# Four edits to the second block of a four-layer kernel: where its stand-by products, splits, statistics and weight sums lie

## The chip, the core and the metric

The kernel runs on one core of one Trainium2 chip. The time is device microseconds for one execution. The kernel before has three timed runs: 600.94 us as their median, 597.98 us the lowest, 601.21 us the highest. Lower is better.

The engines of a core run side by side and wait for each other with semaphores: TensorE (PE; its weight loads are PEld), VectorE (DVE), ScalarE (ACT), GpSimd (POOL) and SyncE (SP), which issues most DMAs. PE writes into eight PSUM banks of 128x512 f32. Each engine goes through its own list in order.

## The reference, cut to what matters

x has 2048 tokens (4 batches of 512) of 128 numbers, in 16 tiles of 128 tokens. Four layers follow each other, each a cross attention to 32 context tokens per batch and a feed-forward part:

```
x = x + L0_xattn(ln(x));  x = x + L0_ffn(ln(x))    # top-2 of 8 experts, GELU
x = x + L1_xattn(ln(x));  x = x + L1_ffn(ln(x))    # top-2 of 8 experts, ReLU
x = x + L2_xattn(ln(x));  x = x + L2_ffn(ln(x))    # quantised weights, convolution, SiLU
x = x + L3_xattn(ln(x));  x = x + L3_ffn(ln(x))    # top-2 of 8 experts, SiLU gate
```

The change lies in layer 1. Its attention is one head of 128: scores of the tokens against the context's keys, softmax over 32, and the sum of the values. Its experts are computed for every token and weighted by a gate G that is zero except for the two chosen:

```
h = relu(einsum('th,ehf->etf', xf, W1) + b1[:, None, :])
y = einsum('etf,efh->eth', h, W2) + b2[:, None, :]
out = einsum('te,eth->th', gate, y)
```

Layer 2's feed-forward part scales each weight matrix by the mean of its absolute values before it rounds it to -1, 0 or 1:

```
scale = 1.0 / jnp.clip(jnp.mean(jnp.abs(w)), 1e-05)
return jnp.clip(jnp.round(w * scale), -1, 1) / scale
```

## The kernel before, in words

`experts(0)` ends layer 0 with a loop over tiles sorted by expert. Then `second_block()`, which each engine has in its own version, does layer 1 and the whole attention of layer 2. The order of each engine's work is written out by hand; nothing is planned or moved by a scheduler.

The second block works in two halves of eight tiles. The first half goes through layer 1's attention before the dense part starts: DVE normalises (`ln_scale` raises `xa_ready`), PE turns the tiles (`tokens1`), ACT copies them to SBUF, PE makes scores (`scores1`), DVE and ACT the softmax (`scores1`, `exponents1`, `shares1`), PE turns the shares and multiplies by the values (`turns1`, `values1`), and DVE adds the result to X (`add1`, two times 128x512). Between these PE makes keys and values of layer 2 (`projected`, `summed`).

DVE then normalises X again for the dense experts, and PE turns these tiles into banks 4 and 5 (`tokens_d`). The products with W1 are made in three passes of a rounded part and a rest, so the tokens are needed as two parts too: `high` (ACT, rounded copy of the bank into XHL), `whole` (ACT, plain copy of the bank into XTF, which the trace calls gb), and `low` (DVE, whole minus high). Of these, `up_d` needs high and low, and `logits_d` (the gate's product) needs the two whole copies of its half.

The dense part is 32 units, `u = 0..31`: group `u // 8` of four tiles, expert `u % 8`. In unit u PE does `up_d(u)` (six 128x512 passes, lines 2016 to 2018), then what the list has at that unit, then `down_d(u-1)` (line 2027, sixteen records). ACT does `hidden1(u)` (ReLU), and DVE `combine1(u)` (line 1602, adds gate times result to X). The second half's attention and its tokens for the dense part are placed among units 2 to 15: its turned tokens come in at units 5 (`tokens1(2)`, `tokens1(3)`) and 14 (`tokens_d(2)`, `tokens_d(3)`), its logits at unit 15.

The means of layer 2's weights are three steps: DVE sums absolute values (`weight_sums`, two reductions), PE adds over the partitions into bank 7, and DVE reads bank 7 (`weight_scales`, which raises `fs_read` twice). POOL waits for `fs_read` 2 and then prepares the weights for layer 2; PE waits for the end of that (`fs_ready`) ahead of layer 2's feed-forward part only.

## Time and profile before

| | us |
|---|---|
| median of three runs | 600.94 |
| lowest, highest | 597.98, 601.21 |
| the profiled execution | 604.28 |
| its span | 602.5 |
| PE busy in the span | 543.9 (90%) |
| DVE busy | 401.4 (67%) |
| ACT busy | 239.3 (40%) |
| POOL busy | 280.1 (46%) |

The span runs from the first to the last instruction of the profiled execution, and 1.78 us of its time lie around it. The execution is 3.34 us above the median of the timed runs. The granted clock of TensorE was 0.949 of full speed on average over the span. The second block starts at about 186 us, its units run from 208 to about 342 us.

A timeline row reads: start, duration, engine, line, operation, output and inputs, shapes, how many, and in brackets how long the engine idled before it and what ended that. PE's ends are modelled and overlap with the next record, so the time that a group takes of PE is better read from start to start. A matmul in f32 shows as two records, a transpose as one.

### The profile page before, as it was taken

To read this page: it belongs to the slowest core of one execution; us is meant where nothing else is said; L and a number is where in the kernel's file an instruction comes from. 1 tells how busy PE (TensorE), PEld (TensorE's weight loads), DVE (VectorE), ACT (ScalarE), POOL (GpSimd) and SP (SyncE) were. 2 spreads that over 40 slices of the span, in tenths; PEclk is the share of its full clock that TensorE was granted. 3 is DMA by queue.
4 is the path that set the end of the run, shared out by engine and by line. 5 is a ranking of instruction groups with operands and counts; after the bars stand their busy time and mean duration, and the time that the engine had idled before them with its cause. 6 is when DMAs were issued, how large, how long until landed. Compare 5 with 4: busy or idle time off the path is not lost.

```text
span 602.5 us, 12300 instructions
## 1 busy us (share of the span) xinstructions
PE 543.9 (90%) x3794; PEld 458.7 (76%) x3809; DVE 401.4 (67%) x1443; ACT 239.3 (40%) x551; POOL 280.1 (46%) x521
## 2 busy tenths in 40 slices
PE   5999984769999799999999999999996897999992
PEld 3678744669997498889987877767773697899992
DVE  8978853333356795465789899988887654555573
ACT  3555503345553543434444334365521222343330
POOL 4474378867657106910000050664526688644332
PEclk9999865999998999989999999999998798999997
DMA  9999012222253100000000450004001222111233
GB/s 302 377 328 274 13 53 67 68 62 75 71 167 104 64 1 1 2 0 1 1 2 0 141 140 2 1 1 141 1 1 45 67 70 58 54 46 52 79 110 122
DMA packets 48153, 47.65 MB, mean 79 GB/s; under 512 B 6471, under 2 KB 37604, under 8 KB 47943
## 3 DMA queue, kind: packets, MB, share of 16 engines
q1 hardware_dynamic: 43558, 37.68, 21.3%
q0 software_dynamic: 4544, 9.38, 4.7%
q8 instruction: 22, 0.36, 0.2%
q14 instruction: 29, 0.23, 0.1%
HBM read 27.53 MB, written 19.51 MB: 78 GB/s over the span
## 4 chain that ended last, share of the span: by engine, by line
PE 58%; DVE 18%; issue 11%; SPq 8%; ACT 2%; another core or an unknown queue 1%; DMA 1%; DVEq 0%; POOL 0%; POOLq 0%; ACTq 0%
PE bank L2453 18%; PE bank L2466 10%; PE bank L2027 7%; SPq L474 4%; SPq L468 2%; PE bank L2016 2%; PE bank L2017 2%; PE bank L2018 2%; PE bank L2441 2%; PE bank L2310 2%; PE bank L2223 2%; SPq L463 1%; PE bank L2268 1%; DVE X L1602 1%
## 5 line engine op out<-in xcount | busy, mean ns | idle before, releaser
L2453 PE MATMUL bank<-xT,wcur 128*128 128x128 f32 x936 | 122.7, 282 | 14.1 <-ACT xT L903 10.5
L2453 PEld LDWEIGHTS bank<-xT,wcur 128*128 128x128 f32 x936 | 114.6, 197 | 17.3 <-issue 9.4
L706 POOL DMA_INDIRECT yt<-Y,dest_i x62 | 60.3, 973 | 59.6 <-ACT Y L919 39.3
L645 POOL TENSOR_SCALAR var_eps<-mv 128x4 f32<-128x4 f32 (+2 forms) x12 | 2.9, 238 | 165.4 <-DVEq L1846 93.5
L690 POOL DMA_INDIRECT xw<-XW,slot_i x64 | 63.1, 986 | 24.6 <-issue 13.0
L1458 DVE COPY wcur<-WA 128x512 f32 x78 | 35.2, 452 | 51.1 <-PE bank L2453 37.3
L987 ACT ACTIVATE hT<-bank,b_cols 128x512 f32<-128x512 f32 x64 | 44.0, 688 | 61.4 <-PE bank L2018 60.8
L2027 PE MATMUL bank<-WC,hT 128*128 128x128 f32 x512 | 64.4, 281 | 0.0
L2027 PEld LDWEIGHTS bank<-WC,hT 128*128 128x128 f32 x512 | 62.0, 196 | 1.6 <-issue 0.2
L1473 DVE TENSOR_TENSOR hT<-gb,bank 128x512 f32<-128x512 f32 x39 | 26.8, 688 | 50.5 <-ACT gb L908 44.2
L1602 DVE SCALAR_TENSOR_TENSOR X<-bank,G,X 128x128 f32<-128x128 f32 x128 | 35.9, 345 | 29.9 <-PE bank L2027 23.5
L908 ACT ACTIVATE gb<-bank 128x512 f32<-128x512 f32 x39 | 23.3, 598 | 54.8 <-PE bank L2453 49.3
L2466 PE MATMUL bank<-WB,hT 128*128 x312 | 41.7, 276 | 0.4 <-issue 0.2
L2466 PE MATMUL bank<-WA,hT 128*128 x312 | 40.9, 275 | 0.0
L2466 PEld LDWEIGHTS bank<-WB,hT 128*128 128x128 f32 x312 | 38.2, 192 | 1.0 <-issue 0.9
L2466 PEld LDWEIGHTS bank<-WA,hT 128*128 128x128 f32 x312 | 37.8, 192 | 0.0
L2268 PE MATMUL bank<-M,XT 128*128 128x512 f32 x64 | 34.9, 628 | 0.1
L908 ACT ACTIVATE hT<-bank 128x512 f32<-128x512 f32 x39 | 23.3, 598 | 27.4 <-PE bank L2453 20.9
L2310 PE MATMUL bank<-VB,YT 128*128 128x36 f32 x256 | 31.9, 271 | 0.0
L2310 PEld LDWEIGHTS bank<-VB,YT 128*128 128x128 f32 x256 | 31.1, 192 | 0.4
L826 ACT ACTIVATE YT<-YT 128x512 f32<-128x512 f32 x32 | 20.2, 632 | 24.4 <-DVE YT L1255 24.4
L919 ACT ACTIVATE Y<-bank 128x128 f32<-128x128 f32 x62 | 17.3, 279 | 31.8 <-PE bank L2466 23.7
(407 smaller groups left out, 1185.6 us busy)
## 6 DMA issues: line engine op xcount, KB each, us to landing
xw<-pad_rows SPq DMA_DIRECT2D x34, 260.0 KB, 4.2
xrow<-xw SPq DMA_DIRECT2D x78, 65.0 KB
WA<-in_fc_dram SPq DMA_DIRECT2D x16, 256.0 KB, 4.3
YT<-yt SPq DMA_DIRECT2D x16, 256.0 KB, 3.2
WA<-in_pj_dram SPq DMA_DIRECT2D x8, 256.0 KB, 5.9
WB<-in_fc_dram SPq DMA_DIRECT2D x8, 256.0 KB, 5.3
WB<-in_pj_dram SPq DMA_DIRECT2D x8, 256.0 KB, 6.5
X<-in_x_dram SPq DMA_DIRECT2D x2, 512.0 KB, 4.2
```

Source lines behind the costliest of these rows:

```text
L690: pool.indirect_dma_start(out=xw_dram, out_offset=bass.IndirectOffsetOnAxis(ap=slot_i[:, choice, tile:tile + 1], axis=0), in_=XW[:, tile, ...
L706: pool.indirect_dma_start(out=yt_dram, out_offset=bass.IndirectOffsetOnAxis(ap=dest_i[:, t:t + 1], axis=0), in_=y_slot(layer, t), in_offse ...
L908: act.activation(dst[:, 0:nc_f, :], bank[s % 2][:, 0:f].rearrange("p (c t) -> p c t", c=nc_f), L["act"]).then_inc(ex_act, 1)
L987: act.activation(hT[F1C * (u % 2) + c][:, :, :], four(bank[F1C * (u % 2) + c]), ACT.Relu, bias=b1_cols[:, F1C * e + c:F1C * e + c + 1]).th ...
L1458: ins = dve.tensor_copy(wcur[:, t % RING, i * width:(i + 1) * width], w[:, bass.ds(e, 1), :].rearrange("p a f -> p (a f)"))
L1473: dve.tensor_tensor(hT[s][:, :, :], gb[:, s % 2, :, :], bank[2 + s % 2][:, :].rearrange("p (c t) -> p c t", c=4), ALU.mult).then_inc(ex_mu ...
L1602: dve.scalar_tensor_tensor(out=X[:, t, :], in0=bank[4 + u % 2][:, j * D:(j + 1) * D], scalar=G[:, t, e:e + 1], in1=X[:, t, :], op0=ALU.mul ...
L2027: ins = pe.matmul(bank[4 + u % 2][:, j * D:(j + 1) * D], hT[F1C * (u % 2) + c][:, j, :], DOWN1[:, e, c * D:(c + 1) * D], start=(c == 0), s ...
L2268: pe.matmul(bank[s % 2][:, :], XT[:, s, :], M[:, b, :], start=True, stop=False)
L2310: ins = pe.matmul(bank[4 + j % 2][:, c * VW:(c + 1) * VW], PT[:, j % 2, c, :], VB[:, b, c, :], start=True, stop=True)
L2453: ins = pe.matmul(dst, wcur[:, s4, at:at + P], xT[s4 % 2][:, :], start=True, stop=True)
L2466: ins = pe.matmul(y, hT[s4][:, c, :], dn[:, bass.ds(e, 1), c * P:(c + 1) * P].rearrange("p a d -> p (a d)"), start=(c == 0), stop=(c == nc ...
```

## The change

1. PE does four more products of ones (`warm(4, 3)`, 128x512 bf16 into bank 3, which nobody reads) at the head of the second block, behind the last products of the loop and ahead of the first wait for `xa_ready`.
2. `low` reads the turned tokens from their PSUM bank, and waits for `xd_high` and no longer for `xd_out`. `whole` now waits for the `low` of the same group (`xd_low`). On ACT, the two `high` come first and then the two `whole`, in both halves.
3. At the head, DVE's statistics of the first four tiles (`ln_stats`) come between `add1(0)` and `add1(1)`, those of the other four behind `add1(1)`.
4. DVE's `weight_sums` moves from ahead of `gates1(0)` to unit 3, `weight_scales` from unit 3 to unit 6 behind `shares1(1)`. PE's product of the sums moves from unit 3 to unit 6 behind `scores1(1)`. PE's wait for `fs_read` moves from ahead of `tokens1(3)` (unit 5) to ahead of `turns1(2)` (unit 9).

```
             def whole(i, src):
+                act.wait_ge(xd_low, i + 1)
                 act.activation(XTF[:, i % 2 * BT:(i % 2 + 1) * BT, :], four(src), ACT.Copy).then_inc(xd_out, 1)
...
                 for i in range(2):
                     high(i, bank[4 + i])
+                for i in range(2):
                     whole(i, bank[4 + i])
...
                     if u == 14:
                         high(2, bank[6])
+                        high(3, bank[7])
                         whole(2, bank[6])
-                        high(3, bank[7])
                         whole(3, bank[7])
...
             def low(i):
-                dve.wait_ge(xd_out, i + 1)
-                dve.tensor_tensor(XLO[i], XTF[:, i % 2 * BT:(i % 2 + 1) * BT, :].rearrange("p t c -> p (t c)"),
-                                  XH[i].bitcast(F32), ALU.subtract).then_inc(xd_low, 1)
+                dve.wait_ge(xd_high, i + 1)
+                dve.tensor_tensor(XLO[i], bank[4 + i][:, :], XH[i].bitcast(F32), ALU.subtract).then_inc(xd_low, 1)
...
-                add1(0, bank[3])
-                add1(1, bank[0])
-                dve.wait_ge(a1_added, GB)
-                layer_norm(half(0), XNR[:, 0:GT, :], xd_ready)
+                for b, src in ((0, 3), (1, 0)):
+                    add1(b, bank[src])
+                    dve.wait_ge(a1_added, b + 1)
+                    ln_stats(everything[b * BT:(b + 1) * BT], b * BT)
+                ln_aggregate(half(0))
+                ln_rstd(GT)
+                ln_scale(half(0), XNR[:, 0:GT, :], xd_ready)
...
-                weight_sums()
                 gates1(0, bank[5])
...
                     if u == 3:
-                        weight_scales()
+                        weight_sums()
...
                     if u == 6:
                         shares1(1)
+                        weight_scales()
...
             def second_block():
+                warm(4, 3)
                 for b in range(GB):
...
-                    if u == 3:
-                        weight_sums()
                     if u == 5:
                         pe.wait_ge(s2_act, 9)
                         tokens1(2, bank[6])
-                        pe.wait_ge(fs_read, 1)
                         tokens1(3, bank[7])
                     if u == 6:
                         scores1(1, bank[6])
+                        weight_sums()
                     if u == 9:
+                        pe.wait_ge(fs_read, 1)
                         turns1(2, bank[7])
```

The next two pieces show ACT's list at units 14 and 15, with the waits of each row. XHL is the rounded copy (`high`), gb the whole one, hT the hidden layer of `hidden1`. First the kernel before:

```order
L987 ACTIVATE hT0<-bank0,b1_cols 128x512 [waits d_dn,d_up]
L987 ACTIVATE hT1<-bank1,b1_cols 128x512 [waits d_dn,d_up]
L972 ACTIVATE XHL<-bank6 128x512 [waits xd_mm]
L975 ACTIVATE gb<-bank6 128x512
L972 ACTIVATE XHL<-bank7 128x512 [waits xd_mm]
L975 ACTIVATE gb<-bank7 128x512
L987 ACTIVATE hT2<-bank2,b1_cols 128x512 [waits d_dn,d_up]
L987 ACTIVATE hT3<-bank3,b1_cols 128x512 [waits d_dn,d_up]
```

And the changed kernel at the same place:

```order
L988 ACTIVATE hT0<-bank0,b1_cols 128x512 [waits d_dn,d_up]
L988 ACTIVATE hT1<-bank1,b1_cols 128x512 [waits d_dn,d_up]
L972 ACTIVATE XHL<-bank6 128x512 [waits xd_mm]
L972 ACTIVATE XHL<-bank7 128x512 [waits xd_mm]
L976 ACTIVATE gb<-bank6 128x512 [waits xd_low]
L976 ACTIVATE gb<-bank7 128x512 [waits xd_low]
L988 ACTIVATE hT2<-bank2,b1_cols 128x512 [waits d_dn,d_up]
L988 ACTIVATE hT3<-bank3,b1_cols 128x512 [waits d_dn,d_up]
```

The whole copies now stand behind both rounded ones and wait for DVE; the hidden rows of unit 15 stay behind them.

On PE, these rows of the kernel before are the ends of unit 5's first products, the turned tokens of the second half, and the head of `down_d(4)`:

```order
L2018 MATMUL bank3<-XHL,W1L 128x512
L1967 MATMUL bank6<-ident,XW 128x128 [waits xa_ready,s2_act]
L1967 MATMUL bank6<-ident,XW 128x128 [waits xa_ready] x3
L1967 MATMUL bank7<-ident,XW 128x128 [waits xa_ready,fs_read]
L1967 MATMUL bank7<-ident,XW 128x128 [waits xa_ready] x3
L2027 MATMUL bank4<-WC,hT0 128x128 [waits d_added,d_act]
```

The changed kernel has there:

```order
L2022 MATMUL bank3<-XHL,W1L 128x512
L1971 MATMUL bank6<-ident,XW 128x128 [waits xa_ready,s2_act]
L1971 MATMUL bank6<-ident,XW 128x128 [waits xa_ready] x3
L1971 MATMUL bank7<-ident,XW 128x128 [waits xa_ready] x4
L2031 MATMUL bank4<-WC,hT0 128x128 [waits d_added,d_act]
```

The wait for `fs_read` has left the second four transposes.

## Rows read from the trace of the kernel before

**Rows 1.** The page, its first line.

```profile
span 602.5 us, 12300 instructions
```

**Rows 2.** Timeline of DVE, second sum and statistics: start, us, engine, line, operation.

```profile
199.51 0.69 DVE L1571 TENSOR_TENSOR X<-X,bank 128x512 f32<-128x512 f32 x1 [0.20 <-PE bank L1987]
200.23 1.65 DVE L1122 BATCH_NORM_STATS2 stats<-X 128x6 f32<-128x128 f32 x8
```

**Rows 3.** Timeline of ACT, the two rounded copies ahead of unit 0.

```profile
206.34 0.60 ACT L972 ACTIVATE XHL<-bank 128x512 fp32r<-128x512 f32 x1 [0.68 <-PE bank L1993]
...
207.37 0.60 ACT L972 ACTIVATE XHL<-bank 128x512 fp32r<-128x512 f32 x1
```

**Rows 4.** Timeline of DVE, the first `low`.

```profile
207.46 0.69 DVE L1575 TENSOR_TENSOR XHL<-gb,XHL 128x512 fp32r<-128x512 f32 x1 [0.51 <-ACT gb L975]
```

**Rows 5.** Timeline of PE, head of unit 0 and its logits.

```profile
208.41 0.47 PE L2016 MATMUL bank<-XHL,W1H 128*128 128x512 f32 x1 [1.08 <-DVE XHL L1575]
...
210.76 1.85 PE L2001 MATMUL bank<-w,gb 128*128 128x8 f32 x16
```

**Rows 6.** Timeline of PE, unit 5: turned tokens of the second half.

```profile
228.70 0.60 PE L1967 MATMUL bank<-ident,XW 128*128 128x128 f32 x4
230.67 0.66 PE L1967 MATMUL bank<-ident,XW 128*128 128x128 f32 x4 [1.38 <-DVE wmean L1626]
231.16 1.95 PE L2027 MATMUL bank<-WC,hT 128*128 128x128 f32 x16
```

**Rows 7.** Timeline of DVE: a weight sum, and the scaling of the second half.

```profile
213.67 0.69 DVE L1620 TENSOR_REDUCE wmean<-w_s 128x1 f32<-128x512 f32 x1 [0.16 <-DVE X L1528]
...
227.38 2.14 DVE L1146 TENSOR_SCALAR XW<-X,mv,rstd 128x128 f32<-128x128 f32 x8
```

**Rows 8.** Timeline of PE, units 14 and 15: turned tokens, `down_d(13)`, logits.

```profile
269.62 1.03 PE L1993 MATMUL bank<-ident,XW 128*128 128x128 f32 x8
270.50 1.95 PE L2027 MATMUL bank<-WC,hT 128*128 128x128 f32 x16
...
273.68 1.85 PE L2001 MATMUL bank<-w,gb 128*128 128x8 f32 x16
```

**Rows 9.** Timeline of DVE, `combine1(13)` and the two `low` behind it.

```profile
272.48 1.13 DVE L1602 SCALAR_TENSOR_TENSOR X<-bank,G,X 128x128 f32<-128x128 f32 x4 [2.94 <-PE bank L2027]
273.52 1.28 DVE L1575 TENSOR_TENSOR XHL<-gb,XHL 128x512 fp32r<-128x512 f32 x2
```

**Rows 10.** Timeline of POOL: head of the weights' preparation, and one piece of it.

```profile
230.93 0.70 POOL L784 TENSOR_SCALAR w_s<-w_s,wmean 128x512 f32<-128x512 f32 x1 [32.15 <-DVE wmean L1628]
...
239.90 1.27 POOL L791 TENSOR_TENSOR Z<-w_s,Z 128x512 f32<-128x512 f32 x1
```

**Rows 11.** Timeline of DVE: the same subtraction in each half, and `combine1(11)`.

```profile
193.24 0.59 DVE L1557 TENSOR_TENSOR WC<-WC,l_max 128x256 f32<-128x256 f32 x1
...
240.07 1.38 DVE L1557 TENSOR_TENSOR WC<-WC,l_max 128x256 f32<-128x256 f32 x1
...
265.31 1.13 DVE L1602 SCALAR_TENSOR_TENSOR X<-bank,G,X 128x128 f32<-128x128 f32 x4 [3.47 <-PE bank L2027]
```

**Rows 12.** Timeline of PE, head of the second block and the second pair of projections.

```profile
187.19 2.26 PE L1967 MATMUL bank<-ident,XW 128*128 128x128 f32 x8 [0.94 <-DVE XW L1146]
...
192.03 3.76 PE L2052 MATMUL bank<-wkv_s,w 128*128 128x512 f32 x4
...
199.40 1.98 PE L2052 MATMUL bank<-wkv_s,w 128*128 128x512 f32 x4
```

**Rows 13.** Stretches of PE: us, busy (records), granted clock, DMA share, GB/s.

```profile
190.00:191.00 1.00, 1.00 (x7) 0.50 0.00 0
...
262.00:264.00 2.00, 2.00 (x11) 0.50 0.00 0
```

**Rows 14.** Groups by line, 200 to 420 us: products of ones.

```profile
L1907 PE MATMUL bank<-ones_bf 128*128 128x512 bf16 x6 | 1.5, 379 | 0.0
```

**Rows 15.** Timeline of PE, `down_d(11)` at the lower clock.

```profile
261.53 3.67 PE L2027 MATMUL bank<-WC,hT 128*128 128x128 f32 x16
```

More of the change, by code:

```diff
@@ L974, in whole @@
             def whole(i, src):
+                act.wait_ge(xd_low, i + 1)
                 act.activation(XTF[:, i % 2 * BT:(i % 2 + 1) * BT, :], four(src), ACT.Copy).then_inc(xd_out, 1)
@@ L1008, in second_block @@
                     high(i, bank[4 + i])
+                for i in range(2):
                     whole(i, bank[4 + i])
@@ L1031, in second_block @@
                         high(2, bank[6])
+                        high(3, bank[7])
                         whole(2, bank[6])
-                        high(3, bank[7])
                         whole(3, bank[7])
@@ L1573, in low @@
             def low(i):
-                dve.wait_ge(xd_out, i + 1)
-                dve.tensor_tensor(XLO[i], XTF[:, i % 2 * BT:(i % 2 + 1) * BT, :].rearrange("p t c -> p (t c)"),
-                                  XH[i].bitcast(F32), ALU.subtract).then_inc(xd_low, 1)
+                dve.wait_ge(xd_high, i + 1)
+                dve.tensor_tensor(XLO[i], bank[4 + i][:, :], XH[i].bitcast(F32), ALU.subtract).then_inc(xd_low, 1)
             def gates1(g, src):
@@ L1632, in second_block @@
                 shares1(0)
-                add1(0, bank[3])
-                add1(1, bank[0])
-                dve.wait_ge(a1_added, GB)
-                layer_norm(half(0), XNR[:, 0:GT, :], xd_ready)
+                for b, src in ((0, 3), (1, 0)):
+                    add1(b, bank[src])
+                    dve.wait_ge(a1_added, b + 1)
+                    ln_stats(everything[b * BT:(b + 1) * BT], b * BT)
+                ln_aggregate(half(0))
+                ln_rstd(GT)
+                ln_scale(half(0), XNR[:, 0:GT, :], xd_ready)
                 low(0)
@@ L1640, in second_block @@
                 combine_second(0, 1)
-                weight_sums()
                 gates1(0, bank[5])
@@ L1652, in second_block @@
                     if u == 3:
-                        weight_scales()
+                        weight_sums()
                     if u == 5:
@@ L1657, in second_block @@
                         shares1(1)
+                        weight_scales()
                     if u == 9:
@@ L2113, in second_block @@
             def second_block():
+                warm(4, 3)
                 for b in range(GB):
@@ L2136, in second_block @@
                         pe.wait_ge(d_read, 1)
-                    if u == 3:
-                        weight_sums()
                     if u == 5:
@@ L2141, in second_block @@
                         tokens1(2, bank[6])
-                        pe.wait_ge(fs_read, 1)
                         tokens1(3, bank[7])
@@ L2145, in second_block @@
                         scores1(1, bank[6])
+                        weight_sums()
                     if u == 9:
+                        pe.wait_ge(fs_read, 1)
                         turns1(2, bank[7])
```

## The prediction

> **What bounds the kernel now.** I read the page first, for the span of 602.5 us [rows 1], then who waited for whom on PE between 180 and 345 us, then the chain of waits over the same stretch, and last the timelines of PE, DVE and ACT. The reader is to see that the second block runs as one chain. Ahead of unit 0 it goes back and forth between DVE, ACT and PE; from unit 0 on it is PE alone, whose records follow each other without a gap except at a few places. So a microsecond of DVE, ACT or POOL counts there only where PE waits for it, and one that PE loses or gains at such a place goes through to the end: the transfers that follow are issued behind results of this chain. Two waits of PE in this stretch are touched: 1.08 us ahead of unit 0, for the first low part [rows 5], and 1.38 us in unit 5, put down to DVE's reading of the weight sums [rows 6]. And there is a place with no wait today that the change makes into one: the logits of unit 15 [rows 8].
>
> The time of the profiled execution is 604.28 us, 1.78 us more than its span. The sum below is made against it; the median of the runs is 3.34 us lower, and I carry the difference over to 600.94 us. A difference under 0.5% (3.0 us) is what a measurement of this kernel can't tell from none.
>
> **Statistics between the sums.** DVE sat idle for 0.20 us between the two additions and then did eight statistics in 1.65 us [rows 2]. Four of them (0.82 us) now start in that hole, and the second addition comes behind them. All instructions stay, only the hole closes, less one more hand-over of about 0.03 us: a gain of 0.15 us, bounds 0 and 0.20 us.
>
> **Low parts from PSUM.** The first rounded copy ends at 206.34 + 0.60 = 206.94 us [rows 3], and DVE is free at 207.46 - 0.51 = 206.95 us [rows 4]. Today `low(0)` starts at 207.46 us since it waits for the whole copy. It will start at about 206.98 us: 0.48 us sooner. A 128x512 addition with one operand in PSUM took 0.69 us [rows 2], and so did `low` with two in SBUF [rows 4], so its length stays. PE's head of unit 0 follows `low(0)` and moves by the same 0.48 us; its turned tokens are in the banks before that. With the statistics, PE starts unit 0 0.6 us earlier (bounds 0.4 and 0.7). The whole copies go to the back: whole 1 waits for `low(1)`, which waits for the second rounded copy (ends 207.37 + 0.60 = 207.97 us [rows 3]), so about 207.97 + 0.03 + 0.69 + 0.05 + 0.60 = 209.35 us. The first logits need it at 210.76 - 0.6 = 210.2 us [rows 5]: hidden, with 0.8 us to spare.
>
> The Trainium skill (VectorE: DVE Perf Modes, on the TRN2 errata) gives a DVE operation a fixed part that is 62 cycles, 0.065 us, longer with its source in PSUM than in SBUF. By it this gain would be 0.42 us; the rows above show no such difference, so 0.48 us stays.
>
> **Weight sums among units.** The two reductions, 0.69 us each and about 1.3 us together [rows 7], leave the place ahead of the gates. DVE is late at that time, so its scaling of the second half, which ends at 227.38 + 2.14 = 229.52 us [rows 7], comes 1.3 us sooner. The two reductions then stand in unit 3 and the reading in unit 6, where DVE waits for PE anyway. PE turned four tiles at 228.70 us, waited, turned the other four and began `down_d(4)` at 231.16 us: 2.46 us from start to start. In unit 14 the same eight took 270.50 - 269.62 = 0.88 us [rows 8]. With no wait for `fs_read`, and the scaling done by 228.2 us, unit 5 takes 0.88 us too, so PE gains 1.6 us (lower bound 1.2 us, if only the part up to 229.52 us goes; upper bound 1.6). PE's small product moves from unit 3 to unit 6: nothing. The wait for `fs_read` at unit 9 comes three units after DVE's reading in unit 6: nothing.
>
> POOL's preparation starts at 230.93 us [rows 10] and moves from unit 3's end to unit 6's; its result is read in layer 2's feed-forward part, long after. But it comes to lie beside DVE's statistics and scaling of units 9 to 12. One subtraction took 1.38 us instead of 0.59 us while POOL's product was at work [rows 10, 11]. Ahead of unit 11's `combine1` DVE idles 3.47 us [rows 11], so one or two such stretches of 0.8 us are hidden: zero, and 0.8 us as upper bound.
>
> The Trainium skill (GPSIMD Engine Reference, Specifications) says that POOL shares its SBUF interfaces with VectorE and that instructions with two SBUF inputs contend; the two rows of the subtraction agree. By it `low` from PSUM, with one SBUF input, would no longer be exposed. It changes no term.
>
> **The whole copies of the second half.** This is the term that speaks against the change. In unit 14 today ACT makes all four copies as soon as the tokens are turned, so PE finds them done at 273.68 us [rows 8]. Now the whole copies wait for `low(2)` and `low(3)`, and these have not moved: on DVE they stand behind `combine1(13)`, which starts at 272.48 us since it waits for `down_d(13)`, and run from 273.52 to 274.80 us [rows 9]. The first low ends at about 274.2 us, whole 2 at 274.85, whole 3, with 0.60 us a copy, at 275.45 us. PE's logits wait for it: 275.5 us in place of 273.68 us, a loss of 1.8 us (bounds 1.6 and 2.1). Behind the waiting copies on ACT stand the hidden rows of unit 15, to about 276.8 us; PE wants them in unit 16, after the logits and `down_d(14)`, so that costs nothing more. Behind the waiting logits on PE stands everything else of the block.
>
> **The products of ones.** Before the head of the second block PE idled 0.94 us, then turned eight tiles in 2.26 us at the pace of DVE's scaling [rows 12]. After that its granted clock fell to 0.50, the level of 1.2 GHz [rows 13], and four 128x512 records took 3.76 us that took 1.98 us at the upper level [rows 12]. Six products of ones took 1.5 us [rows 14], so four take 1.0 us. They fill the gap of 0.94 us, and at most 0.1 us sticks out, which the pace of DVE swallows: cost zero. Whether they keep the clock up is not in the trace. If they do, the keys' product ends 1.8 us sooner and what follows, with the shares now the last to come, follows by 1.8 us. Bounds: 0 and 1.8 us gain. The clock fell also at 261.5 us with PE never idle [rows 13, 15], so gaps are not its only cause, and the turned tokens stay sparse; I take 0.
>
> The Trainium skill (TensorE: Matmul & The Clock Gate, the part on the HAM clock gate) says that the clock follows how busy PE was of late. By it ones in the gap make a fall less likely, which is the second case below.
>
> **The sum.** -0.6 - 1.6 + 1.8 = -0.4 us: 603.9 us for an execution like the profiled one, 600.5 us against the median.
>
> **The rivals.**
> - The ones hold the clock at the head. For it: the fall came right behind the gap. Against it: PE's work there stays thin up to the keys. -0.4 - 1.8 = -2.2 us: 598.7 us.
> - The clock falls behind the new gap, the case on the slower side. PE would idle 1.8 us and then do sixteen records of only eight columns (1.85 us [rows 8]). For it: the fall at the head came after 0.94 us of idling and thin work. Against it: around unit 0 there were 1.08 us of idling [rows 5] with no fall. `down_d` at the lower clock took 3.67 us, not 1.95 us [rows 15, 8], so one such fall costs 1.7 us: +1.3 us, 602.2 us. It decides whenever the ones don't win the same sum back.
> - No new gap: the whole copies come in time after all, and the change does just what it says. For it: the first half, where they do. Against it: the place of `low(2)` in DVE's list. -0.6 - 1.6 = -2.2 us: 598.7 us, or 596.9 us with the clock held.
> - POOL's work, moved to units 7 to 14, holds DVE up by more than it idles, and PE waits for scaled tiles in unit 14. For it: 1.38 against 0.59 us. Against it: DVE's 3.47 us of slack. +0.8 us on the sum: 601.3 us.
>
> **How the numbers follow.** Chances: forecast 0.42; clock held 0.27; clock lost in the new gap 0.16; no new gap 0.10; POOL 0.05. The timed runs of before spread over 3.2 us by themselves, so each case carries about 1.5 us to either side. The range from 597.3 to 603.2 us takes in the clock held below and the clock lost above. Faster by over 0.5% (under 597.9 us): the last part of "no new gap" and the lower edge of "clock held", 0.17. Slower by over 0.5% (above 603.9 us): the upper edge of "clock lost", 0.09. Within: 0.74.
>
> **What would show it.** PE's head of unit 0 should follow the first rounded copy by about 1.0 us, where it was 1.47 us. In unit 5 the eight turned tokens should follow each other. In unit 15 there should be an idle of PE of 1.8 us ahead of the logits, ended by ACT's whole copy, with ACT itself waiting for `low`. The granted clock between 190 and 197 us shows what the ones did, that behind unit 15 what the gap did. Wrong would be: no wait ahead of the logits of unit 15, or a wait still left in unit 5.

## The result, and the profile after

| | before | after |
|---|---|---|
| median of the runs compared, us | 599.46 (4) | 607.1 (4) |
| ratio after to before, 95% interval | | 1.0125 [1.008, 1.017] |
| the profiled execution, us | 604.28 | 605.64 |
| its span | 602.5 | 603.9 |

The changed kernel is slower by 1.25%, about 7.5 us. The forecast was 600.5 us with a range up to 603.2 us, and 0.09 for slower by over 0.5%. It was wrong. On some chips a few executions of every kernel take over 1.5% longer than its fastest; no ratio and no row below is taken from such an execution.

The page's first line, which answers to [rows 1]:

```profile
span 603.9 us, 12309 instructions
```

The span is only 1.4 us longer, but that hides the loss: the part behind the second block took 251.7 us here and 258.4 in the profile of before. It took between 246 and 259 us in the profiles of this study, in kernels that don't differ there, so it says nothing about the change. I therefore cut PE's timeline and compare the stretches between the cuts. "Head" runs from the end of the first loop to the first `up_d(0)`.

| us | head | `up_d(0)` to `down_d(4)` | to `down_d(13)` | to the logits of unit 15 | to the first tile turned behind the block | sum |
|---|---|---|---|---|---|---|
| before | 22.2 | 22.7 | 39.3 | 3.2 | 70.4 | 157.9 |
| after | 23.7 | 20.9 | 42.4 | 6.3 | 70.6 | 164.0 |

So the block is 6.1 us longer, and the loss sits in the third and the fourth stretch, with some in the head. The second gains.

Timeline of PE after, unit 5, where [rows 6] had a wait:

```profile
232.07 1.03 PE L1971 MATMUL bank<-ident,XW 128*128 128x128 f32 x8
232.94 1.95 PE L2031 MATMUL bank<-WC,hT 128*128 128x128 f32 x16
```

All eight tiles in a row, 0.87 us from start to start instead of 2.46. This is as forecast. Timeline of PE after, units 14 and 15, which answers to [rows 8]:

```profile
272.07 0.30 PE L1997 MATMUL bank<-ident,XW 128*128 128x128 f32 x1 [1.91 <-DVE XW L1148]
274.18 1.39 PE L1997 MATMUL bank<-ident,XW 128*128 128x128 f32 x7 [1.81 <-DVE XW L1148]
275.37 3.26 PE L2031 MATMUL bank<-WC,hT 128*128 128x128 f32 x16
...
281.67 1.95 PE L2005 MATMUL bank<-w,gb 128*128 128x8 f32 x16 [1.65 <-ACT gb L976]
```

Two waits for DVE's scaled tokens, 1.91 and 1.81 us, stand where there was none. `down_d(13)` takes 3.26 us instead of 1.95, and then comes the wait for the whole copies, 1.65 us. Stretches of PE after (us, busy, then granted clock, DMA share, GB/s):

```profile
272.00:274.00 2.00, 0.30 (x1) 0.14 (x1) 2.00 (x3) 0.00 (x0) 1.73 (x1) 1.00 0.00 0
274.00:276.00 2.00, 1.82 (x10) 1.76 (x11) 1.93 (x8) 0.99 (x2) 0.00 (x0) 0.67 0.00 0
276.00:278.00 2.00, 2.00 (x12) 2.00 (x11) 0.00 (x0) 0.21 (x1) 0.00 (x0) 0.50 0.00 0
```

Behind the wait the clock went to the level of 1.2 GHz. Why DVE was late is in its own timeline after, around the square root of the normalization:

```profile
261.64 0.98 DVE L1136 TENSOR_SCALAR var_eps<-mv 128x8 f32<-128x8 f32 x1
...
264.71 0.17 DVE L1141 TENSOR_TENSOR y_squared<-rstd 128x8 f32<-128x8 f32 x1
264.91 4.36 DVE L1142 SCALAR_TENSOR_TENSOR minus_half_vyy<-var_eps,y_squared 128x8 f32<-128x8 f32 x1
...
271.16 3.74 DVE L1148 TENSOR_SCALAR XW<-X,mv,rstd 128x128 f32<-128x128 f32 x8
```

An operation on 128x8 elements stands for 4.36 us; its neighbour of the same size in the row above takes 0.17. The scaling takes 3.74 us; it took 2.14 [rows 7]. Timeline of POOL after, at that time:

```profile
263.38 1.28 POOL L793 TENSOR_TENSOR w1c_l<-Z,w1c_h 128x512 fp32r<-128x512 f32 x1
264.74 7.10 POOL L796 TENSOR_SCALAR mfill<-WC 35x2048 bf16<-35x2048 int32 x1
271.90 1.83 POOL L797 MEMSET mfill<- 3x2048 bf16 x1
```

Behind the weights' preparation POOL makes a mask for layer 2, in one operation of 7.10 us, and fills three rows of it with ones in a memset of 1.83 us. The reader is to see that DVE's operation starts 0.17 us behind the first. The memset lies beside the scaling; the timeline of DVE after for 271.9 to 273.7 us alone:

```profile
271.16 2.72 DVE L1148 TENSOR_SCALAR XW<-X,mv,rstd 128x128 f32<-128x128 f32 x4
```

The first four of the eight scalings take 2.72 us, the other four only 1.0 us more. The first four end at 273.88 us, 0.15 us behind the memset's end, and PE's second wait ends at 274.18 us, 0.45 us behind it. So the long operation makes PE's first wait, and the memset most of the longer scaling and the second wait. In the trace of before the same operation stands here:

```profile
250.10 7.09 POOL L796 TENSOR_SCALAR mfill<-WC 35x2048 bf16<-35x2048 int32 x1
```

and DVE did this beside it and behind it:

```profile
253.91 1.12 DVE L1602 SCALAR_TENSOR_TENSOR X<-bank,G,X 128x128 f32<-128x128 f32 x4 [4.22 <-PE bank L2027]
254.95 1.27 DVE L1571 TENSOR_TENSOR X<-X,bank 128x512 f32<-128x512 f32 x2
256.26 1.65 DVE L1122 BATCH_NORM_STATS2 stats<-X 128x6 f32<-128x128 f32 x8
...
259.65 0.17 DVE L1134 TENSOR_SCALAR var_eps<-mv 128x8 f32<-128x8 f32 x1
```

Nothing was held: the combines and sums have one operand in PSUM, and the square root came 2.5 us after the long operation and 0.6 us after the memset was done. Counted from the end of the first loop, the fourth edit moved POOL's list some 13 us later, and with it the mask onto the square root.

The head after: timelines of ACT and PE, one row each, which answer to [rows 3, 5].

```profile
210.42 0.60 ACT L972 ACTIVATE XHL<-bank 128x512 fp32r<-128x512 f32 x1 [0.64 <-PE bank L1997]
```

```profile
212.00 0.47 PE L2020 MATMUL bank<-XHL,W1H 128*128 128x512 f32 x1 [0.59 <-DVE XHL L1577]
```

PE starts 0.98 us behind the end of the first rounded copy, as forecast (1.0, was 1.47). From the first of the turned tokens to the start of unit 0 it took 2.72 us (209.28 to 212.00), where it was 3.20. That the head is 1.6 us longer all the same comes from its beginning, where PE waited 1.70 us for ACT's copies of the turned tokens. None of the seven other profiles with the ones in the kernel has that wait, c_after among them, which differs from this kernel by its bound checks only. So the wait is this execution's own. The head of c_after is as long (23.9 us) for another reason: the values, the second projection and the value sum ran at the lower clock there (3.02, 3.78 and 3.56 us, where before had 2.05, 1.98 and 1.98).

### The profile page after: what moved, and what is told of

Its sections match the earlier page's. It is cut to its first block, busy times and chain, and to the rows that moved or that the text cites. A ratio compares the mean times of both kernels' runs of the same rounds, so it can differ in the third digit from the quotient of the medians.

```text
span 603.9 us, 12309 instructions
## 1 busy us (share of the span) xinstructions
PE 546.4 (90%) x3798; PEld 459.9 (76%) x3813; DVE 408.6 (68%) x1443; ACT 236.9 (39%) x551; POOL 281.8 (47%) x521
## 4 chain that ended last, share of the span: by engine, by line
PE 67%; DVE 22%; another core or an unknown queue 4%; issue 3%; ACT 2%; DMA 1%; SPq 0%; POOL 0%; DVEq 0%; POOLq 0%; ACTq 0%
PE bank L2457 18%; PE bank L2470 11%; PE bank L2031 7%; PE bank L2314 4%; PE bank L2272 3%; PE bank L2303 2%; PE bank L2020 2%; PE bank L2021 2%; PE bank L2022 2%; PE bank L2227 1%; PE bank L2445 1%; PE bank L1911 1%; DVE X L1603 1%; DVE minus_half_vyy L1142 1%
## 5 line engine op out<-in xcount | busy, mean ns | idle before, releaser
L2457 PE MATMUL bank<-xT,wcur 128*128 128x128 f32 x936 | 120.9, 280 | 9.4 <-ACT xT L903 6.5
L2457 PEld LDWEIGHTS bank<-xT,wcur 128*128 128x128 f32 x936 | 113.3, 196 | 11.9 <-issue 9.3
L1254 DVE TENSOR_REDUCE smax<-bank 128x16 f32<-128x512 f32 x32 | 22.0, 689 | 12.3 <-PE bank L2274 5.0
```

Of the source, the lines that this page charges most:

```text
L2457: ins = pe.matmul(dst, wcur[:, s4, at:at + P], xT[s4 % 2][:, :], start=True, stop=True)
```

## The experiments

Every kernel here carries 64 bound checks of loaded numbers on SyncE that the two kernels above leave out; `c_before` and `c_after` are the kernels before and after with them and nothing else. Names with a_ start from the changed kernel, names with b_ from the one before. The ratio is always to the kernel before on the same chip. The chips differ (before ran at 575.8 to 604.5 us), so I compare ratios, and microseconds only of kernels run on the same chip. The intervals don't hold all of the doubt: from the medians of all executions c_after would be 1.0118, a_no_ones 1.0078, b_edit4 1.0041 and b_edit4_mid 0.9960.

| kernel | what | ratio | interval |
|---|---|---|---|
| c_before | nothing | 0.9994 | [0.9955, 1.0034] |
| c_after | the whole change | 1.0088 | [1.0051, 1.0125] |
| a_no_ones | change without the ones | 1.0129 | [1.0084, 1.0173] |
| a_weights_back | without edit 4 | 1.0086 | [1.0058, 1.0113] |
| a_copies_back | second half's copies as before | 1.0076 | [1.0050, 1.0102] |
| a_mask_early | mask ahead of POOL's wait | 1.0146 | [1.0095, 1.0196] |
| a_mask_mid | mask in units 3 to 6 | 0.9996 | [0.9947, 1.0046] |
| b_edit4 | edit 4 alone | 1.0073 | [1.0036, 1.0109] |
| b_edit4_mid | edit 4, mask in units 3 to 6 | 0.9974 | [0.9939, 1.0009] |
| b_edit4_split | edit 4, mask in 8 pieces | 0.9986 | [0.9959, 1.0012] |
| b_copies | second half's copies alone | 1.0064 | [1.0016, 1.0111] |
| b_copies_look | the same | 1.0040 | [1.0012, 1.0068] |
| b_copies_order | their order alone | 0.9971 | [0.9927, 1.0015] |
| b_edit3 | low parts, statistics in the head | 0.9972 | [0.9938, 1.0007] |
| b_ones | the ones alone | 0.9983 | [0.9944, 1.0022] |
| head_only | ones and b_edit3 | 1.0038 | [0.9988, 1.0089] |
| best2 | change, mask mid, copies back | 0.9940 | [0.9904, 0.9977] |
| best2_no_ones | the same without ones | 0.9948 | [0.9909, 0.9987] |

The stretches of the block (the same cuts) in the profiles that matter below:

| us | head | to `down_d(4)` | to `down_d(13)` | to the logits | behind them | sum |
|---|---|---|---|---|---|---|
| c_before | 22.7 | 22.9 | 37.7 | 3.2 | 70.4 | 156.9 |
| c_after | 23.9 | 20.9 | 42.8 | 5.8 | 72.1 | 165.5 |
| a_no_ones | 21.4 | 20.9 | 42.8 | 5.9 | 72.1 | 163.1 |
| a_weights_back | 22.5 | 22.3 | 39.3 | 5.0 | 70.5 | 159.7 |
| a_mask_mid | 21.5 | 20.9 | 39.6 | 5.0 | 70.5 | 157.5 |
| b_edit4 | 22.1 | 20.9 | 42.8 | 4.7 | 70.4 | 161.0 |
| b_edit4_mid | 22.0 | 20.9 | 37.9 | 3.2 | 70.4 | 154.5 |
| b_edit4_split | 21.8 | 27.1 | 37.9 | 3.2 | 70.4 | 160.4 |
| b_copies_look | 22.0 | 27.2 | 37.7 | 5.0 | 73.8 | 165.7 |

The first two stretches swing by some microseconds with where the clock falls: the 27 us of the last two kernels, which ran on one chip in one go, hold a second fall in units 0 to 3. The third stretch is 1.6 us longer where the clock fell ahead of unit 14 (before, a_weights_back and a_mask_mid). So one profile is worth no more than that, and the verdicts rest on the ratios.

From b_copies, best2 and best2_no_ones no row is read.

**First, what each part of the change is worth.** c_after:

> The changed kernel with 64 bound checks of the loaded waits put on SyncE, the form that all runs of this study share; nothing else differs. Theory A (the loss lies in the second block): as slow against before as the changed kernel, 1.0125, some 7 us, and in the profile PE waits about 4 us for the scaled tiles of unit 14, 1.7 us for the whole copies of unit 15, and 1.7 us for ACT's copy at the head. Rival (the loss lies in the loops, by chance or by where code lies): the second block takes within 1 us of the 158 us it took before, from the end of the loop to layer 2's first turned tokens.

Measured 1.0088, with waits where the profile after has them: 0.30 and 1.81 us in unit 14 (the first is short since the clock had fallen from 261.6 to 265.0 us and PE came later), 1.65 us for the copies, and a fall of the clock behind the second and the third. The wait of 1.7 us at the head was not there.

a_weights_back undoes the fourth edit:

```
 combine_second(0, 1)
+weight_sums()
 gates1(0, bank[5])
...
-if u == 3: weight_sums()
+if u == 3: weight_scales()
```

> The changed kernel with edit 4 undone (weight sums, their reading and PE's wait where they were before). Theory A1 (POOL's preparation, moved beside DVE's statistics and scaling of units 10 and 11, holds DVE up): DVE's 128x8 operations of unit 10 are back at 0.17 us each, the scaling at 2.1 us, the waits of PE in unit 14 (4.3 us) are gone, the wait of 1.4 us in unit 5 is back: 3 to 4 us faster than the changed kernel. Rival (only the copies and the head cost): 1.6 us slower than the changed kernel.

The wait in unit 14 was gone and 0.93 us were back in unit 5, yet the ratio stayed at 1.0086, where 3 to 4 us were expected back. By the medians, on the same chip, it was 2.5 us faster than c_after. So the fourth edit is not the only loss. The block of its profile is 159.7 us, 2 to 3 us over the two of the kernel before (157.9 and 156.9); that is 0.3 to 0.5%, and the rest of the 0.86% is not found in it. a_copies_back puts the second half's copies back:

```
-                act.wait_ge(xd_low, i + 1)
+                if i < 2:
+                    act.wait_ge(xd_low, i + 1)
```

> The changed kernel with the low parts and whole copies of the second half made as before (in the first half as changed). Theory A2: PE's wait ahead of unit 15's logits goes from 1.65 us to nothing, and the time falls by 1.7 us; the waits in unit 14 stay. Rival: the logits then wait for something else, DVE's or ACT's late work, and the time stays.

No wait ahead of the logits, the two of unit 14 (1.92 and 1.81 us) still there, 1.0076. The 1.7 us expected are 0.3%; the ratio is 0.12% below that of c_after, and the intervals tell that neither from 0.3% nor from nothing.

**The mask moved too early.** a_mask_early puts POOL's mask ahead of its wait for the weights' means:

```
+pool.wait_ge(in_mask3, 16)
+link(pool.tensor_scalar(mfill[0:PARTS + K, :], mask3_i, 0, FILL, ALU.is_equal, ALU.mult))
 pool.wait_ge(fs_read, 2)
```

> The changed kernel with POOL's two mask operations (7.1 and 1.8 us) moved from behind to ahead of its wait for the weight means, where POOL idles. Theory A1, in the form that the long mask operation holds DVE's ports: the 4.36 us that one 128x8 operation of DVE took in unit 10 fall to under 1.2 us, the scaling is back at 2.1 us, PE waits under 1 us in unit 14, and the time falls by 4 to 5 us. Rival (it is the three taps' products, not the mask): DVE stays late by over 3 us and the time falls by under 1.5 us.

It has the highest ratio of all, 1.0146, and it was the most telling run. Its input arrives when DVE normalizes in the head. Timelines of POOL, DVE and PE of that kernel:

```profile
198.75 7.12 POOL L783 TENSOR_SCALAR mfill<-WC 35x2048 bf16<-35x2048 int32 x1 [3.24 <-DMA WC<-in_mask_dram]
205.92 1.79 POOL L784 MEMSET mfill<- 3x2048 bf16 x1
```

```profile
199.07 6.83 DVE L1137 TENSOR_SCALAR var_eps<-mv 128x8 f32<-128x8 f32 x1
205.93 1.82 DVE L1139 TENSOR_SCALAR seed_bits<-var_eps 128x8 int32<-128x8 int32 x1
```

```profile
209.99 2.27 PE L1998 MATMUL bank<-ident,XW 128*128 128x128 f32 x8 [8.93 <-DVE XW L1149]
```

The hold went with the mask to another place. The first 128x8 operation ends at 205.90 us, the mask at 205.87. The second ends at 207.75 us, the memset at 207.71. POOL's operations, not something in unit 14, hold DVE, and here each holds it to its end.

**The controls, and the change repaired.** c_before and a_no_ones:

> The kernel before, with the 64 bound checks of the loaded numbers on SyncE that every kernel of these experiments carries; nothing else differs from before. It prices the checks: if they cost nothing, the ratio to before is 1.000 within 0.3% and the four kernels run so far are 0.8 to 1.5% slow through the change alone, even with most of it undone. My theory: the checks cost 2 to 4 us (SyncE issues the gathers of the weights in the first loop, whose start they delay), so this one reads 594 to 596 beside 591.8, and the control of the change stands 3 to 5 us behind it. Block (end of the first loop to the last layer's first turned tokens) 157 to 159 us as before, no wait of TensorE ahead of unit 14.

No cost of the checks shows (0.9994, at most 0.34% by the interval, or 2.0 us); my theory of 2 to 4 us fell.

```
-                warm(4, 3)
```

> The changed kernel without the ones behind the first loop. Theory (the ones only move the fall of the clock: held through the first scores, it falls when TensorE waits 1.8 us for the shares): head as in before (scores 3.0 us, first projection 3.76 us at 1.2 GHz, values at full clock), unit 0 starts 22.0 to 22.6 us behind the loop beside 23.9 in the control, time 0 to 1.5 us below the control. Rival (the ones hold the clock and gain): unit 0 later than in the control and the time 1 us above it. The waits of TensorE for the scaled tokens in unit 14 stay, 4 us in all.

1.0129, so the ones are not the loss. best2 takes the changed kernel, the second half's copies as before, and the mask behind a wait that ends in unit 3 (`d_added` counts the combines):

```
+pool.wait_ge(d_added, 16)
+link(pool.tensor_scalar(mfill[0:PARTS + K, :], mask3_i, 0, FILL, ALU.is_equal, ALU.mult))
 pool.wait_ge(fs_read, 2)
```

> The changed kernel with GpSimd's mask operations (the one of 7.1 us) put into units 3 to 6, where the vector engine runs only its combines, instead of behind the weight scales, and the second half's whole copies as before. Theory: the operation of 128x8 in the normalization's square root takes about 0.2 us again beside 4.4, the scaling 2.1 beside 3.7, TensorE waits for nothing ahead of unit 14's transposes nor ahead of the logits, and TensorE waits no more for the weight means in unit 5: block 157 to 158 us plus what the head costs, 5 to 6 us below the control of the change. Rival (any combine beside the 7.1 us operation is held as long): TensorE waits 1 to 4 us for a combine in units 3 to 6, and the gain is half that.

> The same as best2 without the ones. If the ones only move the fall of the clock, it is 0 to 1.5 us faster than best2 and the fastest of the four, 1.5 to 2.5 us below the control of before; if they gain, it is about 1 us slower than best2.

0.9940 and 0.9948: both faster than before, by 0.6 and 0.5%, and the best of the study. The ones make no difference that shows.

**One part at a time, on the kernel before.** b_edit4 and b_edit4_mid:

> The kernel before with the fourth edit alone: weight sums of TensorE in unit 6 instead of 3, its wait for them ahead of unit 9, the vector engine's sums in unit 3 and scales in unit 6; head, copies and ones as before. Theory: unit 5 gains 1.6 us (d4 20.9 us behind unit 0 instead of 22.8), GpSimd's 7.1 us operation then holds the square root's 128x8 operation of the vector engine for about 4.3 us and stretches its scaling to 3.7, TensorE waits 1.9 + 1.8 us in unit 14 and runs on at 1.2 GHz for some 4 us: block 2 to 4 us over before, ratio 1.004 to 1.008. Rival (the loss of the whole change sits in the head or the copies): ratio 0.997 to 1.000, no wait in unit 14.

> The same with GpSimd's mask operations in units 3 to 6, ahead of its work on the weight means. Theory: unit 5 keeps its 1.6 us, unit 14 waits for nothing, the square root's operation takes 0.2 us: block 1.5 to 2 us under before, ratio 0.996 to 0.998. Rival (GpSimd's short weight scales hold the vector engine as well): TensorE waits 1 to 2 us in unit 14 and the ratio is 1.000.

1.0073 and 0.9974, both within the numbers of the theory. Timeline of DVE in b_edit4, where the mask starts at 261.62 us:

```profile
261.59 0.17 DVE L1139 TENSOR_TENSOR y_squared<-rstd 128x8 f32<-128x8 f32 x1
261.79 4.36 DVE L1140 SCALAR_TENSOR_TENSOR minus_half_vyy<-var_eps,y_squared 128x8 f32<-128x8 f32 x1
...
268.03 3.74 DVE L1146 TENSOR_SCALAR XW<-X,mv,rstd 128x128 f32<-128x128 f32 x8
```

In b_edit4_mid the timeline of DVE and that of PE at unit 14:

```profile
263.18 0.17 DVE L1141 SCALAR_TENSOR_TENSOR minus_half_vyy<-var_eps,y_squared 128x8 f32<-128x8 f32 x1
...
265.22 2.13 DVE L1147 TENSOR_SCALAR XW<-X,mv,rstd 128x128 f32<-128x128 f32 x8
```

```profile
268.26 1.03 PE L1994 MATMUL bank<-ident,XW 128*128 128x128 f32 x8
```

POOL's two mask operations, moved by some 30 us, are worth 1.0% (1.0073 against 0.9974), some 6 us; by the medians 0.8%. The block is 161.0 us in the one and 154.5 in the other. What is left of edit 4 in the trace is the gain of unit 5; 0.9974 itself can't be told from nothing. Beside the long operation DVE now had combines and the two reductions (0.68 us each), and none of them was held.

> The kernel before with the low parts of the first half taken from PSUM, their whole copies behind them, and the statistics between the values' sums; no ones, second half and weight sums as before. Theory: unit 0 starts 0.6 to 1.2 us earlier (a_no_ones had it 21.4 us behind the loop, before 22.2 to 22.7), the ratio is 0.998 to 1.000. Rival (the head costs what the run with the weights back seemed to lose beyond its copies, some 3 us): ratio 1.005.

> The kernel before with the ones alone behind the first loop. Theory (the ones move the fall of the clock from the first projection to the values and the second projection, where it is as long): ratio 1.000 to 1.002, unit 0 at 22 to 24 us behind the loop, TensorE waits about 1.8 us for the shares. Rival (they gain): unit 0 below 21 us behind the loop and a ratio of 0.997.

0.9972 and 0.9983, neither told from nothing. For the ones, the timelines of PE at the head of c_before and of head_only, which has them:

```profile
188.47 2.36 PE L1967 MATMUL bank<-ident,XW 128*128 128x128 f32 x8 [0.97 <-DVE XW L1146]
190.61 3.46 PE L1974 MATMUL bank<-M,gb 128*128 128x32 f32 x16
193.89 3.66 PE L2052 MATMUL bank<-wkv_s,w 128*128 128x512 f32 x4
...
201.16 1.98 PE L2052 MATMUL bank<-wkv_s,w 128*128 128x512 f32 x4
```

```profile
187.71 1.03 PE L1917 MATMUL bank<-ones_bf 128*128 128x512 bf16 x4
188.84 2.26 PE L1977 MATMUL bank<-ident,XW 128*128 128x128 f32 x8
190.94 1.93 PE L1984 MATMUL bank<-M,gb 128*128 128x32 f32 x16
192.70 1.96 PE L2062 MATMUL bank<-wkv_s,w 128*128 128x512 f32 x4
196.44 1.05 PE L1991 MATMUL bank<-ident,WC 128*32 128x128 f32 x8 [1.77 <-DVE WC L1569]
197.72 3.43 PE L1997 MATMUL bank<-V,hT 32*128 32x128 f32 x16 [0.24 <-ACT hT L967]
201.08 3.78 PE L2062 MATMUL bank<-wkv_s,w 128*128 128x512 f32 x4
```

The scores and the first projection run at full clock, 1.93 and 1.96 us. PE then has to wait 1.77 us for the shares, since DVE and ACT make the softmax no sooner, and now the clock falls, so that the values and the second projection pay. The fall was moved and not removed. So it was in five of the eight profiles with the ones. In the other three (after, a_mask_early, a_mask_mid) the clock fell 4 to 5 us behind the loop, hardly later than in c_before (3.0). The same move as in head_only happened in b_edit3, which has no ones but in whose execution the gap of 0.97 us was not there either. In the profile of the changed kernel itself the clock fell already at the scores.

> The changed kernel's head alone (ones, low parts of the first half from PSUM, statistics between the sums), with the second half's copies and the weight sums as before. Theory: the parts add up, 0.9972 and 0.9983 alone, so 0.995 to 0.999, unit 0 at 22.5 us behind the loop. Rival (together they cost what the run with the weights back lost beyond its copies): 1.003 or more, with rounded copies late at the scalar engine.

1.0038 with an interval that takes in both; it decides nothing.

**The rest: the copies.** The parts did not add up to 1.25%, so b_copies makes the second half's copies as the change has them, b_copies_order only their order, and a_mask_mid is the whole change with the mask in units 3 to 6.

```
+                if i >= 2:
+                    act.wait_ge(xd_low, i + 1)
                 act.activation(XTF[:, i % 2 * BT:(i % 2 + 1) * BT, :], four(src), ACT.Copy).then_inc(xd_out, 1)
```

with `low` of the second half from PSUM.

> The kernel before with the second half's copies alone as the change has them: both rounded copies first, low parts from PSUM, whole copies behind the low parts. Theory (the wait ahead of the logits and nothing more): TensorE waits 1.65 us for the whole copies ahead of unit 15's logits, the block is 1.6 to 1.8 us longer than before's, ratio 1.002 to 1.004, no fall of the clock behind it. Rival (the copies cost the 0.5 to 0.8% that is missing): a fall of the clock in unit 16 or a later wait, block 3.5 us longer, ratio 1.005 to 1.008.

> The kernel before with the scalar engine's four copies of the second half in the order rounded, rounded, whole, whole, the low parts still from the whole copies in SBUF. If the order alone makes the wait, TensorE waits 1 us or more ahead of the logits and the ratio is 1.002 or more; theory (the wait for the low parts makes it): the last whole copy ends where it ended before, no wait ahead of the logits, ratio 1.000.

```
                         high(2, bank[6])
+                        high(3, bank[7])
                         whole(2, bank[6])
-                        high(3, bank[7])
                         whole(3, bank[7])
```

> The whole changed kernel with GpSimd's mask operations moved to units 3 to 6, nothing else. Theory: the wait of unit 14 goes (with the vector engine's square root at 0.2 us), the wait of 1.65 us ahead of the logits stays and no clock fall follows it; block 1.5 to 2 us longer than best2's, ratio 0.996 to 1.001. Rival (the copies cost 0.5 to 0.8% wherever they stand): ratio 1.002 to 1.005.

> The kernel of b_copies again, for its profile. If the clock falls behind the wait ahead of the logits (logits 2.8 and down projection 3.8 us instead of 1.9 and 2.0, block 4 to 5 us longer than before's) the copies cost 0.5 to 0.8%; if it stays at full speed, 1.65 to 1.8 us, 0.3%, and the rest of b_copies' 0.64% was within its interval.

The order makes no wait and shows no cost (0.9971). With the wait for the low parts the ratios are 1.0064 and 1.0040. Timeline of PE in b_copies_look:

```profile
263.10 2.96 PE L2007 MATMUL bank<-w,gb 128*128 128x8 f32 x16 [1.65 <-ACT gb L977]
265.91 3.76 PE L2033 MATMUL bank<-WC,hT 128*128 128x128 f32 x16
```

The gap is 1.65 us, and the clock falls behind it (the granted clock between 264 and 270 us was 0.50): the stretch from `down_d(13)` to the logits takes 5.0 us instead of 3.2, and the one from the logits on 73.8 instead of 70.4. Together 5.2 us. This execution was the slowest of the kernel's twelve, 6.2 us above their median, so its 5.2 us are no measure of the usual case. In a_mask_mid the same wait stands, and nothing falls:

```profile
276.41 1.95 PE L2006 MATMUL bank<-w,gb 128*128 128x8 f32 x16 [1.64 <-ACT gb L977]
278.22 2.03 PE L2032 MATMUL bank<-WC,hT 128*128 128x128 f32 x16
```

It came out at 0.9996, so moving the two mask operations alone turns the whole change from 1.0088 (c_after) and 1.0125 into no difference. Of the seven profiles with this gap, three show a fall behind it (c_after, a_no_ones, b_copies_look) and four don't (after, a_weights_back, a_mask_early, a_mask_mid). An earlier fall is not what decides: in a_mask_mid the clock had been at the lower level from 12 to 9 us ahead of the gap, in a_mask_early not in the 59 us ahead of it, and neither fell behind it. When it falls stays open.

**How POOL holds DVE.** b_edit4_split cuts the mask in eight:

```
-link(pool.tensor_scalar(mfill[0:PARTS + K, :], mask3_i, 0, FILL, ALU.is_equal, ALU.mult))
+for q in range(8):
+    piece = slice(q * B * S // 8, (q + 1) * B * S // 8)
+    link(pool.tensor_scalar(mfill[0:PARTS + K, piece], mask3_i[:, piece], 0, FILL, ALU.is_equal, ALU.mult))
```

> The kernel before with the fourth edit alone and GpSimd's mask operation (35x2048) in eight pieces of 256 columns at the same place. Theory (an operation of the vector engine is held until the GpSimd operation that runs has ended, or has read its input): no operation of 128x8 stands for more than about 1 us beside the pieces, several are held once each, so that the chain of nine is late by 3 to 6 us all the same, and the ratio is 1.004 to 1.010. Rival (the hold is a price of the long operation alone): the chain is late by under 1.5 us, TensorE waits under 1 us in unit 14, ratio 0.998 to 1.002.

The rival was right. Timelines of POOL and DVE in it:

```profile
250.34 9.09 POOL L798 TENSOR_SCALAR mfill<-WC 35x256 bf16<-35x256 int32 x8
```

```profile
250.31 0.17 DVE L1141 TENSOR_TENSOR y_squared<-rstd 128x8 f32<-128x8 f32 x1
250.51 0.25 DVE L1142 SCALAR_TENSOR_TENSOR minus_half_vyy<-var_eps,y_squared 128x8 f32<-128x8 f32 x1
...
252.64 2.39 DVE L1148 TENSOR_SCALAR XW<-X,mv,rstd 128x128 f32<-128x128 f32 x8
```

The meeting is the same to 0.01 us: the operation comes 0.17 us behind the start of POOL's. It takes 0.25 us instead of 4.36, the scaling 2.39 instead of 3.74, and PE doesn't wait in unit 14. The memset now starts at 259.49 us, behind the scaling. POOL pays 9.09 us for 7.10, which nobody waits for. The ratio is 0.9986.

## Why the prediction was wrong

**The failed step: POOL's work moved beside DVE's.** The prediction said "zero, and 0.8 us as upper bound", from a subtraction that took 1.38 us instead of 0.59 us beside POOL [rows 10, 11], and gave the rival 601.3 us and a chance of 0.05. The mechanism was named, and mis-sized. The row gave 0.8 us beside a POOL operation that was only 1.27 us long. The price grows with POOL's operation, and behind the preparation stands one of 7.09 us: it cost 4.2 us of the 6.9 left of it here, and 6.7 of 6.8 in a_mask_early. I took the row for the price of a stretch, followed POOL's list from its head to one piece of it [rows 10], and not to its end. Then 3.47 us of DVE's idle time [rows 11] could not cover it: 4.2 us for the one operation, 0.8, 0.3 and 1.0 us for three others of the chain beside POOL's pieces (these stand in b_edit4_mid too, where PE doesn't wait), 1.6 us for the scaling, most of it beside the memset. PE waited 3.7 us, and the clock fell behind that. Measured: b_edit4 to b_edit4_mid, 1.0%.

The Trainium skill (SBUF — State Buffer, SBUF: two separate sides) has a rule that the prediction did not weigh. VectorE and GpSimd contend for one pair of ports as for an exclusive lock, held for the whole instruction, and it names VectorE's operations with two SBUF inputs as well as those in its two-port modes. By that rule a 7.1 us operation can cost 7 us; less the 3.5 us of idle time and with one fall of the clock (1.7 us) or none, my estimate for the rival would have been 3.6 to 5.3 us. The hold of 6.83 us to the mask's end agrees; that of 4.36 us ended 2.6 us before the end of POOL's record, which the rule does not give.

**The copies of the second half.** The wait was forecast at 1.8 us and is 1.65. The rival beside it, a fall of the clock behind the new gap, was priced at 1.7 us with 0.16. The fall came in three of seven profiles; it cost 1.7 us in c_after and a_no_ones (72.1 us behind the logits in place of 70.4) and 3.4 in b_copies_look. Its size was right in two of three, its chance set low. Timed, the copies cost 0.40 and 0.64%, or 2.3 and 3.8 us: 1.4 and 2.3 times their wait, with intervals that begin at 0.7 and 1.0 us and so take in the wait alone.

**Unit 5.** Forecast a gain of 1.6 us. The stretch up to `down_d(4)` went from 22.7 to 20.9 us, and b_edit4_mid keeps it.

**Low parts and statistics.** PE's start behind the first rounded copy moved by 0.49 us (forecast 0.48); `low` took 0.69 us from PSUM as from SBUF. The four statistics between the sums came as said (0.87 us between two additions of 0.69 us). b_edit3, 0.9972, doesn't contradict 0.6 us and can't confirm it.

**The ones.** Taken at zero. No difference shows in b_ones or in the pair best2 and best2_no_ones, though the intervals of 0.4% to either side would also hold 1.8 us. The rival with a chance of 0.27 (1.8 us gain) was wrong in its second half: where the clock was held, what that gained was lost again behind the wait for the shares.

**The sum.** By the parts alone: +0.73% (b_edit4), +0.40 to +0.64% (copies), -0.28% (b_edit3), -0.17% (b_ones), together 0.7 to 0.9%. The whole was 1.25% and 0.88%, and 1.29% without the ones; the intervals reach down to 0.8, 0.5 and 0.8%. Not settled: what the head is worth. head_only came to 1.0038, while best2, which has the same head, is at 0.9940. And a_weights_back, the change without edit 4, came to 1.0086, where the parts for head and copies give 0.2% at most, or 0.8 to 1.0% if head_only is right about the head; but then the sum for the whole change is too large (1.5 to 1.8%). So the loss by edit 4 and POOL's mask is shown, some 0.7 to 1.0%; the copies are a second part, and the rest stays open.

## What to carry to other kernels

When an edit moves the time at which a helper engine starts, follow its list to the end and lay each operation beside the other engine's new neighbours; price a meeting of POOL and DVE by up to the length of POOL's operation and not by a ratio seen at a shorter one. Cut a long POOL operation into short pieces where DVE has a chain of small operations that PE waits for, or put it where DVE works from PSUM or sums, as here in units 3 to 6. Count a new gap of PE with the fall of the clock that may follow it: here the clock fell behind three of seven gaps of 1.65 us, and the timed cost was 2.3 and 3.8 us.

## What the runs showed of the hardware that was not expected

- An operation of DVE on 128x8 stood 4.36 us in five profiles (after, c_after, a_no_ones, a_copies_back, b_edit4) and 6.83 us in one (a_mask_early) beside a POOL operation of 7.10 us; 128x512 additions with one operand in PSUM and the statistics beside the same operation kept their 0.64 and 0.21 us each (before).
- The same POOL work in eight pieces held it by 0.08 us (0.25 against 0.17, b_edit4_split).
- A POOL memset of 1.79 us, which reads nothing, held a DVE operation with one input for 1.82 us (a_mask_early). The same memset beside the scaling of 128x128 kept two of its records for 1.7 to 1.9 us each, and PE's wait for them ended 0.45 us behind it, in all five profiles with the hold of 4.36 us.
- Work that keeps PE busy through one gap can leave the clock to fall at the next: the level of 1.2 GHz was entered 3 us behind the first loop in c_before and 10 us behind it in head_only, and lasted some 7 us in both. It was so in five of the eight profiles with the ones.
